# A routed mixture of experts in an AdaLN block: outputs scattered into the output tensor, gates gathered beside the rows, and the next item's transposition placed behind gate and up

## The reference

```python
mod = (silu(c) @ wmod).reshape(4, 6, 1, 256)
sa, ca, ga, sb, cb, gb = (mod[:, i] for i in range(6))
ga = (2 * (ga >= 0) - 1) * maximum(abs(ga), 0.25)      # gb in the same way
h = layernorm(x) * (1 + ca) + sa
x = x + ga * attention(h)          # 16 query heads, 4 key/value heads of 16
h = layernorm(x) * (1 + cb) + sb
probs = softmax(h @ router_w.T)    # 8 experts
w = the most probable experts until their sum exceeds 0.9, with their probabilities, else 0
for e in range(8):
    out += w[:, e:e+1] * ((silu(h @ gate_w[e].T) * (h @ up_w[e].T)) @ down_w[e].T)   # 512 hidden
x = x + gb * out
```

## Time and profile before

| | |
|---|---|
| median of three runs | 614.0 us (613.22 to 616.6) |
| time of the profiled execution | 614.37 us |
| its span | 612.6 us |
| TensorE matmul busy | 483.4 us, 79% |
| VectorE busy | 371.3 us, 61% |
| ScalarE busy | 282.5 us, 46% |
| GpSimd busy | 170.9 us, 28% |
| moved by DMA | 42.01 MB |

### The profile page before, as it was taken

How to read it: one execution, slowest core, us unless ns; L and a number is a source line. 1 busy time by engine, 2 the same in 40 slices (tenths; PEclk the granted TensorE clock), 3 DMA queues, 4 the chain that set the end, 5 groups by cost and what they waited for, 6 DMA issues and landing times. The chain is left out here.

```text
span 612.6 us, 10534 instructions
## 1 busy us (share of the span) xinstructions
PE 483.4 (79%) x3498; PEld 351.2 (57%) x3499; DVE 371.3 (61%) x910; ACT 282.5 (46%) x409; POOL 170.9 (28%) x184
## 2 busy tenths in 40 slices
PE   2745978898899789997315599999997998999810
PEld 2333323244344433425215599999997998999810
DVE  4496287669936983567678175665643755465526
ACT  0244669776886788782000244453423543443300
POOL 6104000000000000000000336656665556476440
PEclk9965989998999999987655699999998998999975
DMA  8243100000000010010121134636453446333338
GB/s 291 95 135 117 61 1 1 1 0 2 24 13 1 1 35 1 1 35 1 34 73 35 46 104 98 158 60 164 90 125 61 109 98 151 56 52 60 44 37 271
DMA packets 33815, 42.01 MB, mean 69 GB/s; under 512 B 5620, under 2 KB 26868, under 8 KB 33784
## 3 DMA queue, kind: packets, MB, share of 16 engines
q0 software_dynamic: 10400, 16.22, 14.5%
q1 hardware_dynamic: 23384, 25.39, 13.0%
HBM read 28.14 MB, written 13.46 MB: 68 GB/s over the span
## 5 line engine op out<-in xcount | busy, mean ns | idle before, releaser
L511 ACT ACTIVATE probs<-psS 128x1024 f32<-128x1024 f32 x128 | 124.0, 1023 | 16.3 <-PE psS L1162 16.0
L1340 PE MATMUL psS<-hs_hi,w_hi 128*128 128x256 f32 x400 | 117.5, 294 | 6.9 <-issue 3.9
L1340 PE MATMUL psS<-hs_lo,w_hi 128*128 128x256 f32 x400 | 114.4, 286 | 0.0
L1340 PE MATMUL psS<-hs_hi,w_lo 128*128 128x256 f32 x400 | 114.3, 286 | 0.0
L404 POOL DMA_INDIRECT y_rows<-y_sel,idx_out x50 | 83.4, 1668 | 55.3 <-DVE y_sel L1035 45.0
L1340 PEld LDWEIGHTS psS<-hs_hi,w_hi 128*128 128x128 f32 x400 | 77.5, 194 | 8.4 <-issue 7.7
L1162 PE MATMUL psS<-qT,kT 96*128 96x512 bf16 x256 | 71.7, 393 | 11.1 <-ACT probs L511 9.4
L1340 PEld LDWEIGHTS psS<-hs_lo,w_hi 128*128 128x128 f32 x400 | 77.7, 194 | 0.0
L1340 PEld LDWEIGHTS psS<-hs_hi,w_lo 128*128 128x128 f32 x400 | 77.5, 194 | 0.0
L1271 PE MATMUL psY<-probs,v_aug 128*32 128x512 f32 x512 | 70.8, 626 | 0.0
L369 POOL TENSOR_TENSOR rstd<-var_eps,minus_half 128x4 f32<-128x4 f32 x4 | 4.8, 1195 | 235.2 <-DVE var_eps L764 235.2
(11 more groups left out here) (188 smaller groups left out, 807.6 us busy)
## 6 DMA issues: line engine op xcount, KB each, us to landing
w_in<-gateT SPq DMA_DIRECT2D x8, 512.0 KB
w_in<-upT SPq DMA_DIRECT2D x8, 512.0 KB
w_in<-downT SPq DMA_DIRECT2D x8, 512.0 KB
x_all<-x SPq DMA_DIRECT2D x4, 512.0 KB, 7.9
mod_rows<-mod_table SPq DMA_DIRECT2D x4, 512.0 KB, 7.6
y_rows<-zeros POOLq DMA_DIRECT2D x2, 1024.0 KB
h_rows<-h_nat SPq DMA_DIRECT2D x4, 512.0 KB, 3.0
y_all<-y_rows SPq DMA_DIRECT2D x4, 512.0 KB, 5.7
```

The source lines that it names most:

```text
L511: act.activation(probs[:, gk % 4, 2 * pair:2 * pair + 2, :], psS[:, pair, :, :], ACT.Exp, scale=ATT_SCALE).then_inc(probs_done, 1)
L1340: mm = pe.matmul(ps[:, i * SW:(i + 1) * SW], w, v[:, k, :], start=at == 0, stop=at == 3 * KC - 1)
```

## The change

- `y_rows` and its zeroing are gone. During attention SyncE copies x (with the attention added) of each batch to the output itself, behind the copy of h. The scatters add to the output's rows.
- A row of `h_rows` has 256 more values, the feed-forward gates of its batch: 2,080 bytes. GpSimd writes them once, in four DMAs. The gates are made by `modulate_gates(1)` in the first body of attention. `take_weights` copies weights and gates (`sel`), and `output` multiplies by both in one instruction.
- The read-back, the multiplication, the addition and the store at the end are gone.
- Padding slots no longer name padding rows: tokens that do not keep an expert get the ranks behind those that do (`others`), and they are gathered and scattered with weight 0.
- The constants of routing are made after the roots of the later batches, and only the memsets of `v_aug` are ahead of them.
- In an item, `turn(m + 1)` stands after `gate_up(m, 1)`; ScalarE and VectorE have their order changed to go with it.

The core of the diff:

```diff
-    ROW = C + E
-    PADS = S * P
+    ROW = C + E + C
+    RING = 4
...
# SyncE
                 sp.dma_start(h_rows[bass.ds(b * N, N), 0:C].rearrange("(t p) c -> p t c", p=P),
                              h_nat[:, :, :]).then_inc(h_out, 16)
+                sp.dma_start(out_rows[bass.ds(b * N, N), :].rearrange("(t p) c -> p t c", p=P),
+                             x_all[:, bass.ds(b * TT, TT), :]).then_inc(x2_out, 16)
...
-            sp.wait_ge(modr_done, 3)
-            sp.wait_ge(scattered, ZEROING + 32 * items)
-            for b in range(B):
-                sp.dma_start(y_all[:, b * TT:(b + 1) * TT, :],
-                             y_rows[b * N:(b + 1) * N, :].rearrange("(t p) c -> p t c", p=P)).then_inc(y_in[b], 16)
-            for b in range(B):
-                sp.wait_ge(out_ready, b + 1)
-                sp.dma_start(out[b].rearrange("(t p) c -> p t c", p=P), y_all[:, b * TT:(b + 1) * TT, :]).then_inc(y_out, 16)
-            sp.wait_ge(y_out, 16 * B)
+            sp.wait_ge(x2_out, 16 * B)
+            sp.wait_ge(scattered, GATES + 32 * items)
+            sp.sem_inc(all_landed, 1)
+            sp.wait_ge(all_landed, 1)
...
# GpSimd
-            for m, v in ((v_aug[:, :, :, :, D:YROWS], 0.0), (tie[:, :, :], 1.0), (earlier[:, :], 1.0), (zeros[:, :], 0.0)):
-                pool.memset(m, v).then_inc(zeroed, 1)
-            pool.wait_ge(zeroed, 7)
+            pool.memset(v_aug[:, :, :, :, D:YROWS], 0.0).then_inc(zeroed, 1)
+            pool.wait_ge(zeroed, 4)
+            pool.memset(v_aug[:, :, :, :, D:D + 1], 1.0).then_inc(v_ones, 1)
+            pool.wait_ge(ln1_eps, 2)
+            pool.tensor_tensor(rstd1[:, TT:], var_eps1[:, TT:], minus_half[:, 0:NT - TT], ALU.pow).then_inc(ln1_rstd, 1)
+            for m in (tie, earlier):
+                pool.memset(m[:, :], 1.0).then_inc(zeroed, 1)
+            pool.wait_ge(zeroed, 6)
...
-            pool.iota(token1[:, :, :], [[P, NT], [0, E]], base=1, channel_multiplier=1, **small).then_inc(consts, 1)
-            pool.iota(pad_row[:, :, :, :], [[0, E], [0, TSLOTS // 2], [P, 2]], base=T + 1, channel_multiplier=1,
-                      **small).then_inc(consts, 1)
+            pool.iota(token[:, :, :], [[P, NT], [0, E]], base=0, channel_multiplier=1, **small).then_inc(consts, 1)
             pool.wait_ge(consts, NCONST)
-            pool.wait_ge(ln1_eps, 2)
-            pool.tensor_tensor(rstd1[:, TT:], var_eps1[:, TT:], minus_half[:, 0:NT - TT], ALU.pow).then_inc(ln1_rstd, 1)
...
+            pool.wait_ge(modr_done, 3)
+            for b in range(B):
+                pool.dma_start(h_rows[b * N:(b + 1) * N, C + E:ROW].rearrange("(t p) c -> p t c", p=P),
+                               mod_rows[:, B + b:B + b + 1, :].broadcast_to([P, TT, C])).then_inc(scattered, 16)
...
# ScalarE, body of an item
                 gate(m, 0)
+                round_hidden(m, 0)
+                gate(m, 1)
                 act.wait_ge(up_ps, 2 * m + 2)
                 round_input(m + 1)
-                round_hidden(m, 0)
-                gate(m, 1)
                 round_hidden(m, 1)
...
# VectorE, end of the first body of attention
                     modulate_gates(0, xhat[:, :, :], h_nat[:, :, :])
+                    dve.wait_ge(modr_done, 1)
+                    modulate_gates(1, xhat[:, :, :], h_nat[:, :, :])
...
# VectorE, routing
-            step(dve.tensor_copy(rank_i[:, :, :], rank[:, :, :]))
+            wide = total[:, NT - 1:NT, :].broadcast_to([P, NT, E])
+            step(dve.tensor_tensor(others[:, :, :], token_f[:, :, :], wide, ALU.add))
+            step(dve.scalar_tensor_tensor(out=others[:, :, :], in0=rank[:, :, :], scalar=-2.0, in1=others[:, :, :],
+                                          op0=ALU.mult, op1=ALU.add))
+            step(dve.scalar_tensor_tensor(out=others[:, :, :], in0=keep[:, :, :], scalar=0.0, in1=others[:, :, :],
+                                          op0=ALU.is_equal, op1=ALU.mult))
+            step(dve.tensor_tensor(rank_i[:, :, :], rank[:, :, :], others[:, :, :], ALU.add))
...
-            step(dve.tensor_copy(row_f[:, :, :], row_i[:, :, :]))
-            step(dve.scalar_tensor_tensor(out=row_f[:, :, :], in0=row_f[:, :, :], scalar=1.0, in1=keep[:, :, :],
-                                          op0=ALU.add, op1=ALU.mult))
-            step(dve.tensor_scalar(row_h[:, :, :], row_f[:, :, :].rearrange("p t e -> p e t"), -1.0, None, ALU.add))
+            step(dve.tensor_copy(row_h[:, :, :], row_i[:, :, :].rearrange("p t e -> p e t")))
...
-            step(dve.scalar_tensor_tensor(out=is_pad[:, :, :], in0=lists, scalar=0.0, in1=pads, op0=ALU.is_equal,
-                                          op1=ALU.mult))
-            dve.scalar_tensor_tensor(out=ids_i[:, :, :], in0=lists, scalar=-1.0, in1=is_pad[:, :, :], op0=ALU.add,
-                                     op1=ALU.add).then_inc(rt_step, 1)
-            dve.tensor_scalar(idx_all[:, :].rearrange("p (s k) -> p s k", k=2),
-                              pad_row[:, 0, 0:1, :].broadcast_to([P, S * ITEMS // 2 + TSLOTS, 2]), -1.0, None,
-                              ALU.add).then_inc(idx_ready, 1)
+            dve.tensor_copy(ids_i[:, :, :], lists).then_inc(rt_step, 1)
+            dve.memset(idx_all[:, :], 0).then_inc(idx_ready, 1)
...
# VectorE, items
-                dve.tensor_scalar(w_sel[:, bass.ds(m + 1, 1), :, 1:].rearrange("p o k e -> p (o k) e"), h_sel[:, :, C:ROW], 0.0,
-                                  None, ALU.max).then_inc(w_copied, 1)
+                dve.tensor_scalar(sel[:, bass.ds(m % RING, 1), :, 1:].rearrange("p o k e -> p (o k) e"), h_sel[:, :, C:ROW], 0.0,
+                                  None, ALU.add).then_inc(w_copied, 1)
...
-                    weighed = dve.tensor_scalar(y_sel[:, k, :], psY[:, k, 0:C],
-                                                w_sel[:, bass.ds(m + 1, 1), k, bass.ds(e1, 1)].rearrange("p a b -> p (a b)"),
-                                                None, ALU.mult)
+                    row = sel[:, bass.ds(m % RING, 1), k, :].rearrange("p a c -> p (a c)")
+                    weighed = dve.scalar_tensor_tensor(out=y_sel[:, k, :], in0=psY[:, k, 0:C], scalar=row[:, bass.ds(e1, 1)],
+                                                       in1=row[:, 1 + E:], op0=ALU.mult, op1=ALU.mult)
...
             def body(e, e2, first, m, half):
-                take_weights(m + 1)
                 product(m, 0)
-                split_input(m + 1)
                 split_hidden(m, 0)
+                take_weights(m + 1)
                 product(m, 1)
+                split_input(m + 1)
+                split_hidden(m, 1)
...
-                split_hidden(m, 1)
...
# TensorE
-            pe.wait_ge(consts, NCONST)
+            pe.wait_ge(v_ones, 1)
...
                 gate_up(m, half, 0)
+                gate_up(m, half, 1)
                 turn(m + 1)
-                gate_up(m, half, 1)
```

More of the change, by code:

```diff
@@ L62, in adaln_block @@
         attention_only = ctx.enter_context(ExitStack())
-        h_rows = nc.dram_tensor("h_rows", [T + PADS, ROW], F32)
+        h_rows = nc.dram_tensor("h_rows", [T, ROW], F32)
         mod_table = nc.dram_tensor("mod_table", [B, 4 * C], F32)
-        y_rows = nc.dram_tensor("y_rows", [T + PADS, C], F32)
+        out_rows = out.rearrange("b n c -> (b n) c")
         def sb(name, shape, dt=F32):
@@ L94, in adaln_block @@
         slot_tile = sb("slot_tile", [P, TSLOTS, NT, E], F16)
-        token1 = sb("token1", [P, NT, E], F16)
-        pad_row = sb("pad_row", [P, E, TSLOTS // 2, 2])
+        token = sb("token", [P, NT, E], F16)
+        token_f = sb("token_f", [P, NT, E])
         rt_max = sb("rt_max", [P, NT])
@@ L162, in adaln_block @@
         row_i = sb("row_i", [P, NT, E], I32)
-        row_f = sb("row_f", [P, NT, E])
+        others = sb("others", [P, NT, E])
         tile_h = sb("tile_h", [P, NT, E], F16)
@@ L192, in adaln_block @@
         psM_b = psM[:, :, :].bitcast(BF16)
[L195 to L196 removed]
+        c_in, wmod_in, wmod_rest_in, wattn_in, wrest_in, x0_in, x_in, x2_out, all_landed = sems(
+            "c_in wmod_in wmod_rest_in wattn_in wrest_in x0_in x_in x2_out all_landed")
         w_loaded = [sem(f"w_loaded{n}") for n in range(3)]
[L198 to L201 removed]
+        zeroed, ident_done, v_ones, consts, silu_step, modc_ps, modc_done, modr_ps, row_copied, mod_out, mod_in, gate_step, modr_done = sems(
+            "zeroed ident_done v_ones consts silu_step modc_ps modc_done modr_ps row_copied mod_out mod_in gate_step modr_done")
         (bn1_done, ln1_stats, ln1_eps, ln1_rstd, mods_done, xhat_done, xT_ps, hT_done, qkv_ps, qkv_sb, squared, sq_sum,
@@ L226, in adaln_block @@
         ROUTE_STEPS = 12
-        NCONST = 8
+        NCONST = 6
         FREE = 2
@@ L403, in scatter @@
                 for k in range(S):
-                    pool.indirect_dma_start(y_rows[:, :], bass.IndirectOffsetOnAxis(ap=idx_out[:, k:k + 1], axis=0),
```

(13 more changed lines are left out.)

43 lines of the change are left out of this document (17 added, 26 removed).

## The result

| | before | after |
|---|---|---|
| median | 614.75 us (4 runs, 613.22 to 616.6) | 660.89 us (4 runs, 658.15 to 661.99) |
| ratio, 95% interval | | 1.0744, 1.0711 to 1.0776 |
| profiled execution: time, span | 614.37, 612.6 us | 658.15, 656.4 us |

The account below looks back on a forecast made before the run. The prediction took TensorE to bound the expert loop, about 8.9 us an item. From a 612.6 us span, 612.6 - 17.0 - 5.8 + 0.4 + 3.7 + 1.0 + 0 + 0.5 - 3.4 - 0.6 + 0.5 = 591.9, giving 593.3 us median, range 588.5 to 601.

Parts of the forecast that it names:

- the one on the loop: Expert loop: with the turn 24 matmuls later, down matmuls still cover ScalarE's rounding and the subtraction, 0 per item.
- ScalarE no longer waits: Expert loop: argument against the rival of VectorE late at changes of expert (+3.5 to +8 us, chance 0.14).
- Tail, -17.0: Kernel end: read-back, eight passes and store go; only a 0.3 us SyncE wake follows the last scatter, -17.0 us.
- y_sel at the tail, -0.6: Tail: y_sel no longer starts behind a late product of 0.68 us, -0.6 us, between 0 and -0.7.
- Constants, -5.8 + 0.4: Start of attention: first xhat free of iotas, -5.8 us; iotas then slow the second block's xhat, +0.4 us.
- Gates, +3.7 + 1.0: First attention body: feed-forward gates delay block 2's xhat, +3.7 us; lower TensorE clock after the stall, +1.0 us.
- Routing and copies, 0: Routing's small operations added and removed cancel; four gate copies into h_rows on GpSimd's queue cost nothing: 0.
- First gather, +0.5: First gather: rows grow from 1,056 to 2,080 bytes, +0.5 us, between 0 and 2.9.
- The stall in the loop, -3.4: Expert loop: the one 2.16 us gather wait is absorbed and the slow matmuls behind it recover, -3.4 us.
- Changes of expert, +0.5: Expert loop: at seven changes of expert VectorE's weight split leaves 0.5 us cover, +0.5 us, between 0 and 8.
- GpSimd as the bound: Rival, expert loop: wider gather rows raise GpSimd's cycle to 9.4 us, about +9, 602 us; chance 0.08.
- slower by its issue: Rival, expert loop: gather issue grows with bytes, GpSimd's cycle 10.2 us, +25, 618 us; chance 0.03.

Follow-up runs that it names:

- e1: Changed kernel with ScalarE rounding the first hidden half after both silus and the next input, VectorE's subtractions reordered to match: 602.82 us, ratio 0.9803.
- e2: Kernel before with only the change's new item order on TensorE, ScalarE and VectorE: 647.85 us, ratio 1.0531.
- e4: Changed kernel with only ScalarE's part of e1's reordering: 663.34 us, ratio 1.0787.
- e5: Changed kernel with only VectorE's part of e1's reordering: 635.05 us, ratio 1.0343.
- e6: e1 with the feed-forward gates made in the last body of attention and their four row copies behind the last root: 598.65 us, ratio 0.9756.
- e9: Kernel before with only the routing constants moved behind the second root, VectorE waiting for them behind attention: 611.49 us, ratio 0.9919.
- e10: e1 with both sets of gates and the added 1 made behind the second xhat, routing constants behind the third: 592.91 us, ratio 0.9619.
- e3: Changed kernel with the old item order on all three engines, all else of the change kept: 618.05 us, ratio 1.006.
- e7: Kernel before with only the routing constants moved behind the second root, VectorE still waiting for them ahead of its first body: 613.57 us, ratio 0.9996.

## Why the prediction was wrong

**The step that failed** is the one on the loop: "24 down matmuls still cover ScalarE's rounding of 0.59 us and the subtraction, a pass of 128x512 elements like that of 0.68 us in the earlier trace rows: 0 per item". The durations were right and the cover was counted from the wrong end. I took the rounding to start at the turn. It stands in a list behind `round_hidden(m, 0)`, and that waits for half of the very matmuls that were to cover it. "ScalarE rounds hidden earlier" and, against a rival, "ScalarE no longer waits" said the reverse of what the wait in line 557 of the changed kernel does: an entry can be put earlier, what it waits for can't. I had not asked of each entry that the change moved forward what it waits for and who is queued behind it. Shown by e1, e2, e4 and e5: the order alone makes +34 us without the rest of the change, and both places mended take 58 us back. In place of 0 it was 2.0 us in each of 24 laps and 1.5 more in eight of them, for the clock, 60 us by laps. Against e6, with the order mended, the loop is 57.1 us longer (305.0 and 247.9), and against the kernel before 54.7, because that loop had stalls of its own; the sum had -3.4 - 0.6 + 0.5 there.

**The other steps.**

- *Tail, -17.0:* the passes are gone as forecast, but it brought 13.2. The forecast took 0.3 us behind the last landing; no row stood under that figure. The windows show no engine and no DMA at work in the last 4.9 us of the changed kernel, and in the last 0.8 us of the kernel before (stretch, us, busy us of PE, PEld, DVE, ACT, POOL, granted clock, DMA share, GB/s; the changed kernel first):

```profile
651.30:651.50 0.20, 0.00 (x0) 0.00 (x0) 0.00 (x0) 0.00 (x0) 0.00 (x0) 0.50 0.05 5
651.50:656.40 4.90, 0.00 (x0) 0.00 (x0) 0.00 (x0) 0.00 (x0) 0.00 (x0) 0.50 0.00 0
```

```profile
611.60:611.80 0.20, 0.00 (x0) 0.00 (x0) 0.00 (x0) 0.00 (x0) 0.00 (x0) 0.50 0.49 159
611.80:612.60 0.80, 0.00 (x0) 0.00 (x0) 0.00 (x0) 0.00 (x0) 0.00 (x0) 0.50 0.00 0
```

So 4.1 us more than before pass with nothing at work, and about that much of the forecast 17.0 is missing. What fills these stretches, and whether the scatters at the end bring them, no run shows. "y_sel at the tail, -0.6" can't be separated.

- *Constants, -5.8 + 0.4:* the first xhat took 1.37 us and TensorE began at 12.09 instead of 17.79 us, -5.7. The second took 5.92, but it ended 0.8 us behind `slot_tile` (56.66 and 55.86) and not the 1.4 of the forecast, so TensorE, at 56.88, was not late for it. Here the trace agrees with the Trainium skill (SBUF — State Buffer, "SBUF: two separate sides") on VectorE's two-port modes and GpSimd shutting each other out: 5.92 and 6.79 us (e9) beside the iotas, 1.38 where the iotas came later (e10). e9 gives -3.2 to -6.8 us for the two. Of the lead of 5.5 us that e6 has at the third transposition (114.10 against 119.59), 4.1 are left at the root behind it. The clock fits the loss: TensorE had stood 2.4 us for this xhat in both, and then the granted clock was 0.53 in e6 and 1.00 in the kernel before (e6 first):

```profile
114.10:116.10 2.00, 2.00 (x9) 1.77 (x10) 0.54 (x1) 0.84 (x2) 0.00 (x0) 0.53 0.00 0
```

```profile
119.60:121.60 2.00, 2.00 (x16) 1.32 (x20) 0.53 (x1) 1.24 (x2) 0.00 (x0) 1.00 0.00 0
```

e9 lost 1.4 us in the same place, at 0.68 and then 0.50. The forecast had no term for it.

- *Gates, +3.7 + 1.0:* right, 4.55 against e6: 3.9 at the third transposition (117.98 against 114.10) and 0.7 behind it. TensorE stood 6.50 us for the third xhat (6.2 forecast), and the granted clock was 0.50 from 121 to 122 us and 0.57 in the next microsecond.
- *Routing and copies, 0:* right. From the last root to the second half of the first gather it is 40.4 us before and 40.5 after.
- *First gather, +0.5:* 0.8, inside its bounds.
- *The stall in the loop, -3.4:* hidden in the changed kernel; with the order mended (e6) all gathers behind the first cost TensorE 0.5 us, and the loop from first turn to last scatter is 247.9 us (340.17 to 588.05), 2.4 less than before. So the new place of the turn was worth having: the wide rows need it (e3 against e1).
- *Changes of expert, +0.5:* the forecast looked for VectorE to be late in 7 laps. It was late in all 24, for the other reason. In e6 it was late twice, at the first two items (3.0 us in all), as in the kernel before (3.1), and at no change of expert.
- *GpSimd as the bound, and slower by its issue:* the slower rival had the sign and not the mechanism. The issue did not grow with the bytes (in the loop its median is 0.99 us, 1.04 before), and GpSimd's waits of 96.9 us are for `sel`. The copies whose spread the prediction read the earlier trace rows do meet the scatters: seven of the 26 took 0.32 to 0.54 us instead of 0.16 to 0.24, and each of the seven falls into the issue of a scatter. But that issue took the usual 1.62 us. So it was the copy that got longer there, and not, as the rival's warning has it, the issue.

That e10 lands at 592.91 us, next to 593.3, is chance: its gates are in another place.

## What to carry to other kernels

When an entry moves forward in an engine's list, write down what it waits for and when that is now done: everything behind it inherits the wait, and a wait for a buffer to come free counts as much as one for data. "Covered by n matmuls" needs the moment at which the covered work may start, not only its length. And where two engines hold such entries in the same line, mending one shows nothing, or half: undo both before the theory is dropped.

## What the runs showed of the hardware

A stall in each lap can cost more than itself. With TensorE standing 1.75 us in every lap the granted clock fell to 0.50 for some 3 us in 8 of 24 laps; with 1.5 us (e2) and 1.39 us (e5) a block of 48 took 5.94 us in 23 of 24, and where TensorE did not stand it took 5.68. Why it fell in some laps and not in others with the same stall, these runs don't tell; nor why it fell behind a stall of 2.4 us in e6 and e9 and not in the kernel before and e7. In kernels that end in scatter-adds the last 4.9 to 5.0 us of the span have no engine and no DMA at work (the changed kernel from 651.5 us, e1 from 597.0, e6 from 591.6); in the kernel before, which ends in plain stores, it is 0.8.
